# One zero-filled buffer for query and value blocks, double places for three gates, and expert outputs by predicated copy and f32 matmul

## What is computed

```python
h = tok(x)                                   # 16 x 512 x 128
h = h + attn(layernorm(h))                   # word tokens, window of 17 keys, 8 heads
xt = layernorm(h); top_vals, top_idx = top_k(xt @ router_w + router_b, 2)
rw = softmax(top_vals)
mask[k, e, n] = (top_idx[n, k] == e)         # expert e sees x * mask, zero elsewhere
def step(carry, xt):                         # one of 16 steps, per k and e
    gates = xt @ Wi + h @ Wh + b             # i, f, g, o
    c = sigmoid(f) * c + sigmoid(i) * tanh(g)
    h = sigmoid(o) * tanh(c)
    return (h, c), h @ Wo + bo
y[n] = sum over k, e of mask[k, e, n] * rw[n, k] * out[k, e, n]
result = h + y
```

## Time and profile before

| | |
|---|---|
| three runs | 2004.2 us median, 2003.4 to 2008.6 |
| profiled execution | 2008.6 us, span of its instructions 2006.8 us |
| TensorE matmuls busy | 1857.2 us, 93% |
| VectorE busy | 1679.9 us, 84% |
| ScalarE busy | 1013.8 us, 51% |
| mean granted TensorE clock | 0.962 of full |
| DMA | 57.1 MB, 28 GB/s |

### The profile page before, as it was taken

The page is one execution under the profiler, slowest core; times in us unless marked ns, Lnnn a source line. Parts: engine busy times, 40 slices in busy tenths (PEclk is TensorE's granted clock), DMA queues, the critical chain, the costliest instruction groups (busy, mean ns, idle before and its releaser), DMA issues.

```text
span 2006.8 us, 32570 instructions
## 1 busy us (share of the span) xinstructions
PE 1857.2 (93%) x12858; PEld 1029.0 (51%) x12858; DVE 1679.9 (84%) x3224; ACT 1013.8 (51%) x1099; POOL 71.8 (4%) x43
## 2 busy tenths in 40 slices
PE   3458899999999999999999999999999999999997
PEld 2324455555555555555555555555555555555554
DVE  2658788898988989888898988889888898988876
ACT  3244644545455455545555464454645545554553
POOL 2000000000000000000000000000000000000000
PEclk9668999999999999999999999999999999999998
DMA  3101121101102020110102102020121202012110
GB/s 109 15 25 33 23 38 20 36 12 33 31 23 36 20 39 12 27 37 23 36 7 43 21 23 39 20 36 12 34 29 23 35 21 38 11 27 36 22 27 6
DMA packets 169885, 57.10 MB, mean 28 GB/s; under 512 B 122442, under 2 KB 167356, under 8 KB 169734
## 3 DMA queue, kind: packets, MB, share of 16 engines
q1 hardware_dynamic: 54022, 47.68, 10.7%
q10 hardware_dynamic: 115712, 7.34, 3.5%
HBM read 39.51 MB, written 4.48 MB: 22 GB/s over the span
## 4 chain that ended last, share of the span: by engine, by line
PE 52%; DVE 32%; issue 6%; ACT 4%; ACTq 3%; DMA 2%; SPq 1%; POOL 0%; DVEq 0%
PE gates L467 33%; DVE h L967 5%; PE FA L402 4%; DVE C L956 3%; DVE tmp L947 3%; DVE tmp L952 3%; ACTq L567 3%; DVE xm L927 2%; PE yp L477 2%; DVE Hs L938 2%; DVE tmp L933 2%; DVE xn L732 2%; PE yp L479 2%; PE yp L478 2%; PE FA L387 1%
## 5 line engine op out<-in xcount | busy, mean ns | idle before, releaser
L598 ACT ACTIVATE tmp<-gates,bias_sb 128x1024 f32<-128x1024 f32 x512 | 568.1, 1111 | 603.6 <-PE gates L467 559.3
L467 PE MATMUL gates<-xm,wi_sb 128*128 128x512 f16 x3072 | 769.5, 388 | 8.2 <-DVE xm L927 4.7
L467 PE MATMUL gates<-Hs,wh_sb 128*128 128x512 f16 x2880 | 706.8, 382 | 0.0
L467 PEld LDWEIGHTS gates<-xm,wi_sb 128*128 128x128 f16 x3072 | 293.2, 100 | 336.5 <-issue 49.5
L467 PEld LDWEIGHTS gates<-Hs,wh_sb 128*128 128x128 f16 x2880 | 284.5, 99 | 348.8 <-issue 16.0
L967 DVE SCALAR_TENSOR_TENSOR h<-yp,wy,h 128x128 f32<-128x128 f32 x1024 | 285.9, 342 | 6.9 <-PE yp L479 6.9
L603 ACT ACTIVATE tmp<-C 128x1024 f32<-128x1024 f32 x128 | 135.3, 1057 | 195.4 <-DVE C L956 194.5
L477 PE MATMUL yp<-wo_sb,Hs 128*128 128x128 f16 x1024 | 187.0, 220 | 48.8 <-DVE h L967 48.6
L947 DVE SCALAR_TENSOR_TENSOR tmp<-tmp 128x1024 f32<-128x1024 f32 x120 | 148.2, 1235 | 54.1 <-ACT tmp L598 53.2
L938 DVE SCALAR_TENSOR_TENSOR Hs<-tmp,Hs 128x1024 f16<-128x1024 f32 x128 | 156.3, 1221 | 41.7 <-ACT Hs L607 40.7
L479 PE MATMUL yp<-wo_sb,Hs 128*128 128x128 f16 x1024 | 187.3, 221 | 0.0
(11 more groups left out here) (160 smaller groups left out, 1422.8 us busy)
## 6 DMA issues: line engine op xcount, KB each, us to landing
masks<-mask_scratch SPq DMA_DIRECT2D x128, 256.0 KB, 4.7
vz<-vwin ACTq DMA_DIRECT2D x64, 112.0 KB, 4.4
out_dram<-h SPq DMA_DIRECT2D x16, 256.0 KB, 2.2
qbd<-attn SPq DMA_DIRECT2D x128, 28.0 KB, 1.9
C<-in_wi SPq DMA_DIRECT2D x1, 2048.0 KB, 11.5
C<-in_wh SPq DMA_DIRECT2D x1, 2048.0 KB, 16.2
xm<-in_wo SPq DMA_DIRECT2D x1, 512.0 KB, 14.6
ids<-in_x_ids SPq DMA_DIRECT2D x16, 32.0 KB, 4.8
```

What stands on the lines that cost most here:

```text
L467: last = mm(gates[:, slot, k * SEQ:(k + 1) * SEQ], w, v, start=(n < K), stop=(n >= len(seq) - K))
L598: A(tmp[:, gate, :], gates[:, g % 2, :], ACT.Tanh, bias=bias_sb[:, e, gate:gate + 1], scale=UNSCALE).then_inc(s_tanh, 1)
```

## The change

1. `qbd` and `vz` become one buffer `diag` with the layout of `vz`. The queries are written as `qz`: for each block two columns groups, the queries times a 0/1 parity of the head, so that 4 DMAs of 32 partitions fill the diagonal. SP waits for the values' matmuls of the step before, and ScalarE's DMAs of the values wait for the window's scores of this step. Both memsets become one, written as f32.
2. `tmp` has 7 places: two each for the input, cell and output gates, one for the forget gate, which is also the place of the cell's tanh. The waits of `gate_tanh` reach back accordingly. In step 0, where the cell is zero, the forget gates are not made at all. The last step makes no f16 parts of the hidden state.
3. Outputs: for each expert, `chosen` copies the hidden state of choice 1 over that of choice 0 where the token has this expert as choice 1, by a predicated copy, and multiplies by the token's weight for this expert. One f32 matmul adds it to `yp`, now transposed (features in partitions); a matmul with the weights `wT` starts it with the bias. Once a step, `yp` is copied out (slot 5), turned back by 4 transposes (slot 6) and added to `h2` (slot 7). The mask rows and the weights come by two more broadcast DMAs per expert, after the weights, too, were stored to DRAM.
4. Several small tiles are views of others (`ids` in `prod`, `lg` and `mk` in `pr`), which adds waits: `ids` is loaded behind the last use of `prod`.

```diff
-    sp.wait_ge(S["S"], b)
-    for h in range(HEADS):
-        load(qbd[DH * h:DH * h + DH, h * TF:(h + 1) * TF], qperm[DH * h:DH * h + DH, :], S["qbd"])
+    sp.wait_ge(S["O"], b)
+    for g in range(NG):
+        load(diag[32 * g:32 * g + 32, :, :, g, :]..., qz[32 * g:32 * g + 32, :, :, :, :]..., S["qbd"])
...
-    last = mm(FA[:, r, jj * KB:(jj + 1) * KB], qbd16[:, j::NBLK, qv],
+    last = mm(FA[:, r, jj * KB:(jj + 1) * KB], diag[:, qv, j, :, :].rearrange("p g d -> p (g d)"),
               khl[:, kv, j * QB:j * QB + KB], start=False,
...
+def gate_at(gate, e):
+    return {I: e % 2, G: 2 + e % 2, F: 4, O: 5 + e % 2}[gate]
+TANH_C = gate_at(F, 0)
...
+def rows_in(s, e):
+    if e == 0:
+        sp.wait_ge(S["mout"], (s + 1) * 32)
+    n = s * E + e
+    if n >= 2:
+        sp.wait_ge(s_z, n - 1)
+    sp.dma_start(rowk1[:, e % 2, :], mask_dram[s, E + e:E + e + 1, :].to_broadcast([P, SEQ]))
+    sp.dma_start(roww[:, e % 2, :], mw_dram[s, e:e + 1, :].to_broadcast([P, SEQ]))
...
 # SP's step, slot by slot
+    if g == 3 and e < E - 1:
+        rows_in(s, e + 1)
+    elif g == 3 and not last:
+        rows_in(s + 1, 0)
...
 # SP, slot 28
     load(mask_dram[...], mrow[:, :], S["mout"])
+    sp.wait_ge(S["wT"], b + 1)
+    load(mw_dram[b, :, :], wT, S["mout"])
...
 # gate_tanh
-    if not (first and e == 0):
-        if gate == O:
-            act.wait_ge(s_hlo, s * E + e)
-        else:
-            act.wait_ge(s_c, s * E + e)
+    m = s * E + e
+    if gate == F and m >= 1:
+        act.wait_ge(s_h, m)
+    elif gate == O and m >= 2:
+        act.wait_ge(s_z, m - 1)
+    elif m >= 2:
+        act.wait_ge(s_c, m - 1)
...
-def unit_y(s, e, k, yfirst):
-    pe.wait_ge(s_hlo, s * E + e + 1)
-    if not yfirst:
-        pe.wait_ge(s_yadd, s * (E * K) + e * K + k)
-    (4 tiles of 3 matmuls)
+def unit_y(s, e):                                     # behind slot g = 0 of expert e + 2
+    pe.wait_ge(s_z, s * E + e + 1)
+    mm(yp[:, :], wo_sb[:, e, :], z32[:, :], start=False, stop=(e == E - 1)).then_inc(s_y, 1)
+def y_bias(s):                                        # behind slot 8
+    pe.wait_ge(S["wT"], s + 1)
+    if s:
+        pe.wait_ge(s_yadd, s)
+    mm(yp[:, :], bo_sb[WT0:WT0 + E, :], wT, start=True, stop=False).then_inc(S["ybo"], 1)
...
+def chosen(s, e):                                     # VectorE, slot g = 2 of expert e + 1
+    dve.wait_ge(s_row_in[e % 2], 32 * (s * (E // 2) + e // 2 + 1))
+    dve.wait_ge(s_hlo, n + 1)                         # s_h in the last step
+    at = tmp[:, gate_at(O, e), :]
+    V.copy_predicated(at[:, 0:SEQ], rowk1[:, e % 2, :].bitcast(u16), at[:, SEQ:2 * SEQ]).then_inc(s_sel, 1)
+    if n:
+        dve.wait_ge(s_y, n)
+    dve.wait_ge(s_sel, n + 1)
+    TT(z32[:, :], at[:, 0:SEQ], roww[:, e % 2, :], ALU.mult).then_inc(s_z, 1)
+def add_y(s, par):                                    # slot 7
+    dve.wait_ge(s_yback, s + 1)
+    dve.wait_ge(S["h2"], s + 1)
+    TT(flat, flat, yp[:, :], ALU.add).then_inc(s_yadd, 1)
```

More of the change, by code:

```diff
@@ L321, in step @@
                     e, g = t // NG, t % NG
-                    if t == 8 and not first:
+                    if t == 9 and not first:
                         store(s - 1, 1 - par)
@@ L334, in _ @@
             mask_in(0, 1)
+            rows_in(0, 0)
             run_steps(step)
@@ L437, in front @@
                     for i in range(TILES):
-                        nc.tensor.transpose(FB[0:K * E, i * P:(i + 1) * P], mk[:, i, :], ident[:, :])
-                    for i in range(TILES):
-                        last = nc.tensor.transpose(FA[0:E, 1, i * P:(i + 1) * P], mw[:, i, :], ident[:, :])
+                        last = nc.tensor.transpose(FB[0:WT0 + E, i * P:(i + 1) * P], mkw[:, i, :], ident[:, :])
                     last.then_inc(S["mwp"], 1)
-                if t == PE_AT["bias"]:
-                    pe.wait_ge(S["wT"], b1)
-                    for i in range(TILES):
-                        last = mm(FA[:, 0, i * D:(i + 1) * D], wT[:, i * P:(i + 1) * P], bo_sb[:, :], start=True, stop=True)
-                    last.then_inc(S["bp"], 1)
             def unit_gate(s, e, g, first):
                 gate = ORDER[g]
-                slot = g % 2
-                if not (first and e == 0 and g < 2):
-                    pe.wait_ge(s_tanh, s * (E * NG) + e * NG + g - 1)
+                n = gates_to(s, e, g)
+                slot = (n - 1) % 2
+                if n > 2:
+                    pe.wait_ge(s_tanh, n - 2)
                 if g == 0:
@@ L611, in step @@
                     e, g = t // NG, t % NG
-                    gate_tanh(s, e, g, first)
-                    if g == 0 and e:
+                    if not first or ORDER[g] != F:
+                        gate_tanh(s, e, g, first)
+                    if t == YT_AT and not first:
+                        y_out(s - 1)
+                    if g == 0 and e and not last:
                         split_hi(s, e - 1)
-                    elif g == 0 and not first:
+                    elif g == 0 and not e and not first:
                         split_hi(s - 1, E - 1)
@@ L985, in step @@
                         masked_input(s, e + 1, par, first and e == 0)
-                    if g == 1 and e:
+                    if g == 1 and e and not last:
                         hidden_lo(s, e - 1)
-                    elif g == 1 and not first:
+                    elif g == 1 and not e and not first:
                         hidden_lo(s - 1, E - 1)
@@ L1016, in _ @@
             hidden(STEPS - 1, E - 1)
[L1017 to L1021 removed]
+            chosen(STEPS - 1, E - 1)
+            add_y(STEPS - 1, (STEPS - 1) % 2)
         @block.gpsimd
```

254 lines of the change are left out of this document (135 added, 119 removed).

## The result

| | median us | range | runs |
|---|---|---|---|
| before | 2006.4 | 2003.4 to 2009.4 | 4 |
| after | 1917.8 | 1917.6 to 1918.5 | 4 |

The ratio is 0.956, with a 95% interval of 0.954 to 0.958: 4.4% faster. The forecast was 1876 us (6.4% faster) with a range of 1822 to 1938. The direction and the stated range held; the forecast's own range of 1850 to 1902 did not: a third of the expected gain is missing. The profiled execution of after took 1918.1 us, its span is 1916.3 (before 2008.6 and 2006.8).

The account below looks back on a forecast made before the run. TensorE was taken as the bound on average, VectorE close behind. 14 middle steps at -7.0 us (-98), step 0 -13, start -5, last step -3 and end -9 gave -128: 1876 us on the median's scale, range 1822 to 1938.

Parts of the forecast that it names:

- part A: Step from embedding matmul to output projection: 79.6 us would fall to 74.1, less 1.1 for double places; TensorE stays the bound.
- Window and clock: Window's scores on TensorE: contiguous query blocks save 2.8 us a step, full clock on the gate matmuls behind saves 1.1.
- Rival (c): Window: contiguous weights bring no speed-up, 2.8 + 1.1 us a step come back; period 115.5, total 1928 us; chance 0.08.
- Output units, waits for the adding, VectorE's work: Each step: output units save TensorE 3.4 us at 0.91 each, waits for adding 2.0; VectorE goes from 105.0 to 97.
- Rival (d): VectorE's predicated copy runs at the strided pace, 2.5 us for 512 elements; slower than before, 2047 us; chance 0.08.
- Rival (b): VectorE sets more: copy takes 1.2 us, or ids and rows land 2 to 3 us later; 1930 us; chance 0.14.
- Part B stays at 39: Step from projection to next embedding: a chain of masks, reload and one-hot ends 1.9 us later, so no gain.
- the second store: End of a step: the reload of the masks waits for two stores instead of one, +0.5 us.
- the ids: End of a step: the ids' load queues late on SP, so the one-hot waits for it, +0.9 us.
- Rival (a): New waits at the end of a step are hidden, TensorE sets everything: 109 us a step, 1830 us; chance 0.17.
- Step 0: First step, set by VectorE and latency between engines: no forget gates, shorter addings, double places; -13 us (-5 to -18).
- Start and end: Ahead of step 0: shorter memset and window, -5 us (0 to -8); behind the last gate's tanh: -9 us.

Follow-up runs that it names:

- blocks_only: Kernel before with only the shared zero buffer and contiguous query blocks of the change, output and gate places as before: 1949.2 us, 0.972 of before.
- no_copy: Kernel after without the predicated copy on VectorE, so the second choice's routing is missing from the output: 1863.2 us, 0.930 of before.
- values_by_sync: Kernel after with the four DMAs of the values' blocks issued by SyncE instead of ScalarE: 1901.5 us, 0.948 of before.
- copy_first: Kernel of values_by_sync with ScalarE's copy of the window's probabilities at gate 15 ahead of the cell's tanh: 1889.6 us, 0.942 of before.
- single_places: Kernel after with one place instead of two for each of the gates I, G and O: 1915.7 us, 0.956 of before.

## Why the prediction was right in direction and short in size

- **TensorE first, by the earlier trace rows.** Right for the kernel before: blocks_only gave back 3.8 of 3.9 us. Wrong for part A after the change, where it says that "TensorE keeps the bound": there TensorE waits for tanhs and for VectorE, and no_copy, which changes VectorE's work alone, shortens A by 1.5 us.
- **Window and clock (2.8 and 1.1 us).** Right: 2.49 us, and 3.8 of the 3.9 in the period. Rival (c) is refuted with it: the loads take 96 ns with contiguous blocks against 163 strided. The Trainium skill, "TensorE: Matmul & The Clock Gate", section "Weight-path perf modes — Fast Weight Load (FWL) and DoubleRow", allows the fast load for 16-bit weights at any column step up to 1,024 elements. The strided block, with a step of 56, does not load as fast here; the measurement decides. What the forecast lacks is that the clock drop comes back behind the projection: in 4 of 13 middle periods of after and 6 of blocks_only, 2 before, some 0.3 and 0.5 us a step, in part B.
- **Output units, waits for the adding, VectorE's work.** Right: 0.87 us a unit, no wait left, 98.1 us on VectorE. The work on VectorE was forecast at 97. Rival (d) is refuted: the copy takes 0.73 us. Rival (b) named a period of 115.5 by a copy of 1.2 us or rows that come late; neither is seen.
- **Part B stays at 39.** Right by time (40.0 to 39.4 by the table's cut), and both links are shown: the second store is worth some 0.6 us (forecast 0.5), the ids 0.5 (forecast 0.9, where the terms as listed add up to 1.3). In part the time agrees by compensation: the one-hot waits 0.3 us for the ids, not 1 to 2, and the clock behind the projection, which the forecast lacks, costs 0.3 more. Rival (a), that these waits are hidden, is refuted.
- **Part A at 73 to 74: the step that failed.** The forecast let A fall by 6.6 us with the double places, it fell by 4.6. Two terms were mis-sized. "ScalarE issues them behind a gate's tanh that itself waits for TensorE's unit behind the window, so nothing is added": the issue holds ScalarE 3.1 us and is worth 1.1 us a step (values_by_sync), and a second place of the same kind, the copy ahead of a tanh at gate 15, costs 0.8 (copy_first). And the 1.1 us "of small waits that double places of three gates take away" are nothing (single_places). These are 3.0 us, 1.1 more than the miss of 1.9 a step; the wait ahead of the transpose of x came out 0.4 smaller (0.8 for 1.2), the remaining 0.7 are not traced to a term.
- **Step 0 (13 forecast, 5.0 found).** I counted VectorE's savings in full. no_copy shows that there too a us on VectorE is worth half; single_places (99.8 for 99.2) that the double places give 0.6 at most. The blocks give 1.0 of the 5.0. What else holds step 0 was not tried.
- **Start and end (5 and 9 forecast).** 3.3 and 8.1 found: the steps were right, the start was counted a third too high.

The common cause of the miss: with TensorE's spare waits gone, queues that had been covered came to the surface, and I had looked for that at the transposes and at the end of the step but not at the tanhs, where the trace of before shows no wait of TensorE in a middle step.

## What to carry to other kernels

When a change takes several us off the busiest engine of an in-order pipeline, go through every hand-over to it, those without a wait today above all, and ask how much slack each has; a DMA issue in a compute engine's queue counts as work of that engine. When two engines are near each other (here 108.5 and 98.1 us busy of 113.9), don't price a us on either in full: here it was about half, and work taken off the second can give back no more than the first one's idle time. Before moving an operation ahead of another, see what the second one covers. And compare the busiest engine's busy time at equal work: where it grew, look at its clock.

## What the runs showed of the hardware

- A 512-element product on GpSimd and an operation on VectorE at the same time hold each other up: VectorE's rows went from 1.22 to 2.17 us, GpSimd's from 1.27 to 2.15. The Trainium skill, "SBUF — State Buffer", section "Who interferes with whom", says that a VectorE instruction with two SBUF inputs contends with a GpSimd instruction that reads SBUF. The trace agrees: the cell's first operation ends at 1108.22, GpSimd's product, begun at 1107.19, ends 1.12 us after that, and the cell's second operation is 0.95 us longer, as if each waited for the other's instruction to end.
- An f32 predicated copy of 512 elements with a 16-bit mask takes 0.73 us, little more than an f32 product of the same size (0.69).
- Four DMA issues of ScalarE hold its next operation up by 3.0 to 3.1 us.
- The clock drop behind the window is gone with the shorter window, while behind the f32 projection it appears in 4 of the 13 middle periods (a granted clock of 0.83 over 10 us, six gate matmuls at 2.33 us for 1.46, the whole gate unit at 4.29 for 2.59); before shows it there in 2 of 13. These are two rows of windows of after, the stretch with the window and the one behind the projection, and the gate unit of the second in order of time:

```profile
1155.43:1170.43 15.00, 15.00 (x138) 7.63 (x137) 13.17 (x15) 6.37 (x7) 0.00 (x0) 1.00 0.54 91
1207.43:1217.43 10.00, 10.00 (x41) 4.95 (x41) 8.87 (x21) 3.10 (x3) 1.91 (x1) 0.83 0.05 15
...
1210.48 2.33 PE L506 MATMUL gates<-xm,wi_sb 128*128 128x512 f16 x6
1212.61 2.32 PE L506 MATMUL gates<-Hs,wh_sb 128*128 128x512 f16 x6
```
